# Gated experts in a sixteen-step kernel: a new order of two VectorE operations per tile, and the output biases moved into the routing stage

## The reference, cut to what matters

```
def _L3_ffn_ref(x, router_w, router_b, w1, b1, w2, b2):
    def _expert_ffn(xf, wa, ba, wb, bb):
        h = xf @ wa.T + ba
        h1, h2 = jnp.split(h, 2, axis=-1)
        h = jax.nn.silu(h1) * h2
        return h @ wb.T + bb
    logits = (x @ router_w.T + router_b)
    topk_val, topk_idx = jax.lax.top_k(logits, 2)
    weights = jax.nn.softmax(topk_val, axis=-1)
    # eight experts, hidden width 512; the two chosen ones, weighted, are summed
...
x = x + _L3_attn_a_ref(_layernorm(x), ...)
x = x + _L3_ffn_ref(_layernorm(x), ...)
x = x + _L3_attn_b_ref(_layernorm(x), ...)
x = x + _L3_ffn_ref(_layernorm(x), ...)
```

## Time and profile before

| | |
|---|---|
| median of 3 runs | 6225.26 us (6223.73 to 6227.15) |
| profiled execution | 6223.72 us, its span 6221.8 us |
| PE busy | 3906.2 us (63%), PEld 2459.3 (40%) |
| DVE busy | 3758.3 us (60%) |
| ACT busy | 2448.4 us (39%) |
| POOL busy | 1708.2 us (27%) |
| mean granted TensorE clock | 0.795 |

### The profile page before, as it was taken

How to read it: one execution, slowest core, us unless ns; L and a number is a source line. 1 busy time by engine, 2 the same in 40 slices (tenths; PEclk the granted TensorE clock), 3 DMA queues, 4 the chain that set the end, 5 groups by cost and what they waited for, 6 DMA issues and landing times. The chain is left out here.

```text
span 6221.8 us, 78605 instructions
## 1 busy us (share of the span) xinstructions
PE 3906.2 (63%) x21844; PEld 2459.3 (40%) x21844; DVE 3758.3 (60%) x6990; ACT 2448.4 (39%) x4474; POOL 1708.2 (27%) x1709
## 2 busy tenths in 40 slices
PE   5756648466664488724666664688855847476474
PEld 3546438222233233322222223344434636454464
DVE  4323651599974677544888886655567635566354
ACT  2334226355532277613545443233333524243242
POOL 0043014355542355422333340000001140301412
PEclk8868659688876699856778785799966779887898
DMA  2012003100001222012000000000000011100111
GB/s 82 0 55 75 1 10 91 41 1 0 0 4 54 74 82 89 22 36 79 0 1 0 0 0 2 18 1 0 0 2 2 2 45 41 39 8 2 45 42 51
DMA packets 224866, 170.50 MB, mean 27 GB/s; under 512 B 27435, under 2 KB 211602, under 8 KB 223714
## 3 DMA queue, kind: packets, MB, share of 16 engines
q1 hardware_dynamic: 204130, 125.44, 6.8%
q0 software_dynamic: 20480, 41.98, 2.3%
HBM read 92.02 MB, written 74.45 MB: 27 GB/s over the span
## 5 line engine op out<-in xcount | busy, mean ns | idle before, releaser
L1775 POOL TENSOR_TENSOR XN<-s_l_attn_a_h,LOG 128x512 f32<-128x512 f32 x512 | 642.5, 1276 | 768.6 <-DVE s_l_attn_a_h L1815 753.5
L1815 DVE TENSOR_TENSOR_SCAN s_l_attn_a_h<-s_l_attn_a_da,XN 128x512 f32<-128x512 f32 x512 | 598.5, 1211 | 142.9 <-ACT s_l_attn_a_da L1760 102.7
L1751 PE MATMUL s_l_attn_a_y_ps<-XN,c_ident 128*128 128x512 f32 x1024 | 588.7, 704 | 25.2 <-DVE s_l_attn_a_y L2027 15.4
L1760 ACT ACTIVATE s_l_attn_a_da<-s_l_attn_a_delta,s_l_attn_a_a 128x510 f32<-128x510 f32 x512 | 353.3, 690 | 526.0 <-DVE s_l_attn_a_h L1815 525.5
L483 DVE COPY s_l_ffn_ffn_xt<-s_l_ffn_ffn_turned 128x128 f32<-128x128 f32 x416 | 120.9, 292 | 711.1 <-PE s_l_ffn_ffn_turned L604 709.5
L569 POOL DMA_INDIRECT s_l_ffn_ffn_back<-slots_y,s_l_ffn_ffn_slots x320 | 302.8, 946 | 875.3 <-DMA slots_y<-PICK 566.4
L623 PE MATMUL s_l_ffn_ffn_down<-down,s_l_ffn_ffn_hid 128*128 x2944 | 421.1, 284 | 193.4 <-DVE s_l_ffn_ffn_hid L496 186.0
L623 PEld LDWEIGHTS s_l_ffn_ffn_down<-down,s_l_ffn_ffn_hid 128*128 128x128 f32 x2944 | 361.2, 192 | 233.6 <-issue 228.5
L416 ACT COPY s_l_ffn_ffn_own_w<-up 128x512 f32 (+2 forms) x416 | 305.0, 734 | 375.4 <-DVE s_l_ffn_ffn_expert_no L467 277.3
L1730 PE MATMUL s_l_attn_a_spread<-s_l_attn_a_parts,s_l_attn_a_pick 96*128 96x512 bf16 x512 | 182.2, 443 | 390.3 <-DVE XN L1806 243.2
L561 POOL DMA_INDIRECT slots_x<-XN,s_l_ffn_ffn_slots x320 | 311.5, 973 | 388.9 <-DVE s_l_ffn_ffn_slots L460 293.2
(11 more groups left out here) (631 smaller groups left out, 8651.3 us busy)
## 6 DMA issues: line engine op xcount, KB each, us to landing
XNT<-slots_x SPq DMA_DIRECT2D x32, 640.0 KB, 6.3
slots_y<-LOG SPq DMA_DIRECT2D x16, 640.0 KB, 4.3
slots_y<-PICK SPq DMA_DIRECT2D x16, 640.0 KB, 4.3
s_l_attn_b_qr<-s_l_attn_b_q_rows SPq DMA_DIRECT2D x64, 144.0 KB
s_l_attn_b_kr<-s_l_attn_b_k_rows SPq DMA_DIRECT2D x64, 144.0 KB
XNT<-slots_x SPq DMA_DIRECT2D x8, 768.0 KB, 7.0
slots_x<-PICK SPq DMA_DIRECT2D x10, 512.0 KB, 6.4
slots_x<-XN,s_l_ffn_ffn_slots POOLq DMA_INDIRECT x320, 2.2
```

The costliest lines, as they stand in the source:

```text
L1751: last = self.nc.tensor.matmul(self.y_ps[:, i, :], self.k.ident[:], self.hc[n % 2][:, i, :], start=(n == 0), stop=(n == NST - 1))
L1760: self.nc.scalar.activation(self.da[:, i, :, 1:], self.delta[par][:, i, :].rearrange("p (b t) -> p b t", b=BPG)[:, :, 1:], ACT.Exp, scale= ...
L1775: self.nc.gpsimd.tensor_tensor(self.hc[n % 2][:, i, :], self.h[n % 2][:, i, :], self.c_rows[n % 2], ALU.mult).then_inc(self.hc_ready, 1)
L1815: self.nc.vector.tensor_tensor_scan(self.h[n % 2][:, i, :], self.da[:, i, :, :].rearrange("p b t -> p (b t)"), self.u[n % 2][:, i, :], 0.0 ...
```

## The change

In `sparse_experts`, for the gated experts alone, VectorE's loop does `gate_hid(j-1)` ahead of `shift(j)`. The stage `expert_bias` is gone; what it did is now inside `sparse_experts`: `spread` is GpSimd's first instruction there, the transposes of the gates and the eight products come on TensorE behind the two ranking products, and the eight additions on VectorE behind the gates' reductions and ahead of the first `take_xt`. The products use the PSUM tiles `up` and `up_b`, so they wait until the ranks in them have been read (`slots_used`), and TensorE goes on only when all eight additions are done.

```diff
@@ sparse_experts, declarations
+            gates_t, spread = s.sb("gates_t", [P, 2, P]), s.sb("spread", [P, HT, D])
+            gates_up, gates_turned, spread_ready = s.sem("gates_up"), s.sem("gates_turned"), s.sem("spread_ready")
+            bias_up, bias_added, slots_used = s.sem("bias_up"), s.sem("bias_added"), s.sem("slots_used")
+        bias_ps = [flat(b[:]).rearrange("p (t d) -> p t d", d=D) for b in up + up_b] if gated else None
@@ VectorE
             nc.vector.tensor_copy(slots[:, 0, :], (low if choices == 2 else high)[:]).then_inc(slots_ready, 1)
+            if gated:
+                dve.sem_inc(slots_used, 1)
...
             dve.drain()
+            if gated:
+                for g in range(GROUPS):
+                    dve.wait_ge(bias_up, g + 1)
+                    xg = k.X[:, g * GT:(g + 1) * GT, :]
+                    nc.vector.tensor_tensor(xg, xg, bias_ps[g % 4], ALU.add).then_inc(bias_added, 1)
+                dve.drain()
             for j in range(min(2, NT)):
                 take_xt(j)
             for j in range(NT):
                 if j + 2 < NT:
                     take_xt(j + 2)
                 if gated:
-                    shift(j)
                     if j > 0:
                         gate_hid(j - 1)
+                    shift(j)
@@ ScalarE, ahead of the first take_w1
+            if gated:
+                act.wait_ge(gates_up, 1)
+                for h in range(2):
+                    last = nc.scalar.copy(gates_t[:, h, :], turned[h][:])
+                last.then_inc(gates_turned, 1)
@@ GpSimd, ahead of the sends
+            if gated:
+                nc.gpsimd.tensor_tensor(spread[:],
+                                        k.bufs["L3_ffn_b2"][:].rearrange("p (a d) -> p a d", a=1).to_broadcast([P, HT, D]),
+                                        k.bufs["c_own_tile"][:].rearrange("p (t a) -> p t a", a=1).to_broadcast([P, HT, D]),
+                                        ALU.mult).then_inc(spread_ready, 1)
@@ TensorE, behind the ranking products
+            if gated:
+                for h in range(2):
+                    last = nc.tensor.transpose(turned[h][:], k.GATE[:, h * HT:(h + 1) * HT, :].rearrange("p t e -> p (t e)"), k.ident[:])
+                last.then_inc(gates_up, 1)
+                pe.wait_ge(gates_turned, 1)
+                pe.wait_ge(spread_ready, 1)
+                pe.wait_ge(slots_used, 1)
+                for g in range(GROUPS):
+                    if g >= 4:
+                        pe.wait_ge(bias_added, g - 3)
+                    h, q = divmod(g * GT, HT)
+                    nc.tensor.matmul(bias_ps[g % 4], gates_t[:, h, :], spread[:, q:q + GT, :], start=True, stop=True).then_inc(bias_up, 1)
+                pe.wait_ge(bias_added, GROUPS)
@@ l3_ffn
         softmax8(nc, k, name + "_gate", True, k.bufs["L3_ffn_rb"])
-        expert_bias(nc, k, name + "_bias")
         sparse_experts(nc, k, name + "_ffn", consts, 2, 8, 4, gated=True)
```

More of the change, by code:

```diff
@@ L652, in l0_ffn @@
         sparse_experts(nc, k, name + "_ffn", consts, 2, 4, 4)
[L655 to L699, removed]
 def l3_ffn(nc, k, name):
```

## The result

The kernel after took 5996.48 us (median of 4 runs, 5986.93 to 6005.45), the kernel before 6224.49 (4 runs, 6219.08 to 6227.15): ratio 0.9635, interval 0.9615 to 0.9654, 228 us less. The forecast was 6003. The profiled execution took 6003.23 us, 6.8 over the median.

What follows compares the result with a forecast made beforehand. The prediction took a circle of waits in the gated tiles, down waiting for `hid`, as the bound; 195.5 us from the order plus 26.5 from the biases, 222 off the median of 6225.26, gave 6003 us, range 5970 to 6070 (0.8).

Steps and rivals of the forecast that it cites:

- the circle: Gated tile loop before: down, transpose, copy to `xt`, `shifted_b`, `shifted_a`, `hid`, down again, 4.18 us round.
- The new pace: Gated tile loop after: `hid`, register load, `shifted_b`, `shifted_a`, `silu` set a period of 2.85 us.
- the hand-over from `silu` to `hid`: Gated tile loop after: semaphore term between ScalarE's `silu` and VectorE's `hid`, estimated at 0.05 us.
- the stalls: Gated tile loop: longer idle ahead of `shifted_b`, in every tenth tile and some others, costs 0 to 7 us per pass.
- A: Gated tile loop: TensorE is the bound at 2.78 us a tile, stalls vanish, 5977 us; chance 0.20.
- TensorE over 93% busy: Gated tile loop after: a sign of the forecast, expected with periods of 2.8 to 2.9 us.
- B: Gated tile loop: register load starts only when `hid` is through, 3.45 us, 6098 us; 0.18 including what lies towards the forecast.
- C: Gated tile loop: something unseen keeps the pace at 4.18 us, only the moved biases count, 6199 us; chance 0.05.
- D: Gated tile loop: late `silu` puts all steps in a row, 4.97 us a period, slower at 6324 us; chance 0.05.
- The cover: Routing: the moved bias work fits where VectorE sat idle 42.69 us before the first transposed tile.
- The first send as long after the mask copy as now: Routing after: a sign of the forecast, GpSimd's first send 8 us after the mask copy; later means the hold-up.
- a hold-up of `reach` by `spread`: Routing: GpSimd's `spread` delays VectorE's `reach` by 0 to 1.2 us a pass, taken as 0.6.

Runs made afterwards that it cites:

- Experiment 9: Kernel before with the register load of each gated tile ahead of the copy to `xt` instead of behind it: 6299.93 us, ratio 0.9834.
- experiment 3: Kernel after with the register load of the expert's number ahead of the copy to `xt`: 6175.77 us, ratio 0.9643 to the kernel before.
- Experiment 4: Kernel after with the register load of each gated tile done twice, the second result unused: 6274.46 us, ratio 0.98 to the kernel before.
- experiment 6: Kernel after with `shifted_a` ahead of `shifted_b`, `silu` waiting for `shifted_a` alone: 5985.31 us, ratio 0.9614 to the kernel before.
- experiment 1: Kernel before with only `hid` of tile j-1 moved ahead of the biases of tile j, bias stage kept: 6205.96 us, ratio 0.9692.
- Experiment 2: Kernel after with the old order of VectorE's loop, so only the biases are moved: 6378.28 us, ratio 0.9958 to the kernel before.
- experiment 7: Kernel after with 12 idle TensorE products of 512 columns in every softmax stage: 6014.97 us, ratio 0.966 to the kernel before.
- 12: Kernel after with `shifted_a` first, register load directly behind the biases, `spread` in the normalisation stage, idle products in the two gated softmax stages: 6170.19 us.
- experiment 10: Kernel after with GpSimd's `spread` moved into the normalisation stage before the softmax: 6196.0 us (2 runs), ratio 0.9672 to the kernel before.

## Why the prediction came out right

**The bound of the kernel before.** The list of waits and one tile named the circle, and both were right. Experiment 9 puts a price on what the prediction had as one step of the circle: 0.65 of the 4.18 us were the register load.

**The new pace.** Forecast 2.85, measured 2.83; the one term that differs is the hand-over from `silu` to `hid`, 0.03 instead of the estimated 0.05. The forecast of 232 us a pass was 3.7 too long (228.2 and 228.5): 79 x 0.02 = 1.6 of it are the period. The rest is the stalls. 228.3 less 79 x 2.83 leaves 4.7 us for everything uneven, where 7 were allowed at the upper of the two ends that the prediction kept: a period of about 3.3 in every tenth tile, some 0.5 each for 8 tiles, 0.03 a tile on average with a combine, a little won in the first tiles. The long tiles were the register load's: in every tenth tile it takes up to 0.88 us instead of 0.31 (the row of line 493 above), and with its place on the circle they went away (experiment 3). Why it takes longer there was not looked for.

So the 195.5 us of the order were 7 too few (202.8) and the 26.5 of the biases 1.5 too many (25.0). That the profiled execution took 6003.23 us, just the forecast, is luck: 7.4 us were lost in other stretches, of which the prediction had two as unchanged (from first send to first down product 0.5 and 0.1 us more, behind the last down product of the run 0.5).

**The rivals.** A (TensorE the bound, 5977) lost by 0.04 us a tile. Experiment 4 shows that the circle binds, experiments 3 and 6 that TensorE waits right under it, at 2.79; the kernel that is really bound by TensorE takes 5985 (experiment 6, beside 6005 for the kernel after). A distance this small was not in the prediction's power to call: its own semaphore term, 0.05, was as large. The mark "TensorE over 93% busy" couldn't tell the two apart, since 99.8% also stands at 2.83. B (the load doesn't hide) was wrong as a whole, but 0.25 us of the load do stick out behind `hid`: the forecast had them in its 0.85, taken from a row where the load ran beside a copy of 0.25 us. That the same 0.85 holds behind an operation of 0.60 us was not argued from a row, and in that the prediction was lucky. The queue's rows of the kernel before would have said it: the load starts 0.015 us after the start of the copy in front of it, not after its end, and in the kernel after it does so behind `hid`. C fell with experiment 1. D fell with the list of waits of the kernel after: `hid` waits for `silu` 19 times, 7.2 us in all (the 0.03 us of idle in a plain tile is too short for the list), and `down` for `hid` 4 times, 6.0 us, where the earlier trace rows had 160 times.

**The biases.** Forecast 26.5 us. Experiment 2 measured 25 of 6403.61 (interval 16 to 37), the two profiles 12.30 + 12.68 = 25.0. Of the 1.5 us that are missing, 1.2 were lost in the routing (below); most of the rest is the bias stage of the first pass, 0.4 us shorter than that of the second, which the prediction took for both. The cover held: the 8 additions ran from 5658.47 to 5663.92, within 6 us of the last gates' reduction (5657.93), and VectorE was idle a further 37.3 us before the first `xt`:

```profile
5701.23 0.51 DVE L490 COPY s_l_ffn_ffn_xt<-s_l_ffn_ffn_turned 128x128 f32<-128x128 f32 x2 [37.31 <-PE s_l_ffn_ffn_turned L640]
```

**What was wrong.** "The first send as long after the mask copy as now": it is 1.19 us later, and the step behind it, a hold-up of `reach` by `spread` of 0 to 1.2 us, taken as 0.6, was mis-sized and incomplete. The hold-up is 0.26. The other 0.94 was not foreseen: the bias stage's 8 products had given TensorE the full clock for the ranking. Windows of the ranking products, second pass, in the kernel before and after:

```profile
5764.70:5767.30 2.60, 1.10 (x4) 0.68 (x4) 1.13 (x3) 0.00 (x0) 0.00 (x0) 1.00 0.00 0
```

```profile
5644.50:5647.30 2.80, 2.22 (x6) 1.62 (x6) 0.45 (x2) 0.00 (x0) 2.63 (x1) 0.50 0.00 0
```

Before, TensorE had been idle for 1.58 us, and the granted clock over the products was 1.00, full; after, it has been idle for 14.98 us, and the clock is 0.50, half, 1.2 GHz. (The 0.74 in the expectation of experiment 7 is the mean over the whole routing, in which the clock fell behind the products.) Experiments 7 and 12 gave the clock back and `incl` with it. The four kernels 7, 10, 12 and the one after have every combination of clock and `spread`: `incl` goes by the clock alone (1.75 or 2.69 us behind the mask copy), and `reach` is held only beside `spread`. The Trainium skill (TensorE: Matmul & The Clock Gate, "Part 1: The HAM clock gate") says that half rate is the default and that activity lifts it; the trace agrees. A prediction that takes work off TensorE in front of short products has to ask for this.

The two delays don't add freely. Experiment 7 removes the 0.94 of the clock, and `reach`, which now starts earlier, is held by 1.20 instead of 0.26: the first send comes 9.16 us after the mask copy as before. Either way the price is 1.2 us a pass, the prediction's upper bound, and with the full clock it would have been `spread`'s alone. The rule of the Trainium skill that the prediction weighed (SBUF — State Buffer, "SBUF: two separate sides"), that such an operation waits for GpSimd's whole instruction, would have said 1.2 then. The trace agrees in the main: `reach` ends 0.27 to 0.29 us behind `spread` in both passes of all nine profiles that have them side by side, and isn't held in experiment 10. That is 0.14 less than its own 0.42 us, so it had started, or `spread`'s recorded end is late, by that much; the runs can't say which.

## What to carry to other kernels

Draw the circle of waits of one tile, with every register load and drain as a term of its own, and redraw it for the new order: the sum of start-to-start distances gave the period to 0.02 us. Where the operation written in front of a register load had to wait, the load began with that operation, and the one behind it could start 0.85 us later: on the circle the load cost 0.85 us less the time of the operation in front. Where VectorE's queue was ahead, it cost nothing. Here the best place was directly behind the additions that use the load before, and ahead of any drain. A busy share near 100% doesn't name the bound: TensorE was 99.8% busy at 2.83 us a tile and could do 2.79. When a stage is removed, ask what it did besides its work: here it kept TensorE's clock up and kept GpSimd's work away from VectorE's. Products that are to keep the clock up must be shorter than the stage that hides them.

## What the runs showed of the hardware

- Where the operation in front has to wait (`hid` after, the copy before), the register load on VectorE's queue starts 0.015 us after that operation starts, and the operation behind the load 0.85 us after it. Its place cost 0.65 us a tile in the old circle (experiment 9) and 0.25 in the new (3, where TensorE's bound left 0.04 of it to be won); a second load costs 0.62 (4).
- VectorE's `reach`, two inputs in SBUF, runs to 0.28 us behind the end of GpSimd's `spread`, from two different starts (experiment 7 and the kernel after): 1.63 us and 0.69 us instead of 0.42.
- The two ranking products (four records of 256 columns) after 14.98 us of idle TensorE ran at granted clock 0.50 and delayed the operation behind them by 0.94 us against a clock of 1.00.
- The same code takes 6224 us on one chip and 6404 to 6406 on two others. In the profiles taken on the slower ones single tiles are held up, with either order of the loop: above all the first period of a pass, which lasts 24.7 to 28.2 us in all passes but one, where it is 2.8 to 4.2 on the faster chip, and single periods around tile 43, with up to 8.5 us. VectorE's copy in the first two tiles of experiment 1:

```profile
5179.00 0.29 DVE L483 COPY s_l_ffn_ffn_xt<-s_l_ffn_ffn_turned 128x128 f32<-128x128 f32 x1 [6.05 <-remote]
...
5205.04 0.29 DVE L483 COPY s_l_ffn_ffn_xt<-s_l_ffn_ffn_turned 128x128 f32<-128x128 f32 x1 [23.96 <-remote]
```

  Their cause was not looked for and stays open.
